# A graph network kernel: sums of the message pass kept in PSUM, one-hots made by GpSimd, and the first LayerNorm inside the pass

## What is computed

```python
# x (6250, 256), src/dst/edge_weight (100000,), dst sorted; row = src, col = dst
rbf = exp(-0.5 * ((d[:, None] - centers) / (abs(widths) + 1e-5)) ** 2) * env[:, None]
r = silu(rbf @ rbf_w1 + rbf_b1) @ rbf_w2 + rbf_b2
W = silu(silu(r @ filt_w1 + filt_b1) @ filt_w2 + filt_b2) @ filt_w3 + filt_b3
agg = segment_sum((x[col] @ node_w + node_b) * W, row)          # the message pass
o = layernorm(x + agg) * ln_g + ln_b
x = layernorm(x + o * sigmoid(o @ gate_w + gate_b))             # the node stage
fwd = segment_sum(w * x[col, :128], row) / clip(deg_row, 1)
bwd = segment_sum(w * x[row, 128:], col) / clip(deg_col, 1)
out = layernorm(x + concat([fwd, bwd]))
```

## Time and profile before

| | us |
|---|---|
| median of 3 runs (5069.38 to 5073.18) | 5071.47 |
| the profiled execution | 5067.16 |
| its span, first to last instruction | 5065.1 |

### The profile page before, as it was taken

The page is one execution under the profiler, slowest core; times in us unless marked ns, Lnnn a source line. Parts: engine busy times, 40 slices in busy tenths (PEclk is TensorE's granted clock), DMA queues, the critical chain, the costliest instruction groups (busy, mean ns, idle before and its releaser), DMA issues.

```text
span 5065.1 us, 77985 instructions
## 1 busy us (share of the span) xinstructions
PE 3600.8 (71%) x16432; PEld 2653.5 (52%) x16433; DVE 2815.1 (56%) x7139; ACT 2019.5 (40%) x5492; POOL 3207.5 (63%) x3263
## 2 busy tenths in 40 slices
PE   6999999999999999788875544444443556565662
PEld 4655555555555555466653344444443555555552
DVE  4665656556566565466668522222222666666667
ACT  1555455554555545488884211111111222222221
POOL 0777777777777777600003477777777777777772
PEclk8999999999999999999997655555555776777775
DMA  7544444444444444476661111111111433334334
GB/s 191 134 136 135 135 138 136 137 135 135 137 135 136 135 135 138 137 226 216 215 212 40 32 53 53 53 53 53 53 53 59 113 102 102 102 105 107 102 102 77
DMA packets 464444, 588.32 MB, mean 116 GB/s; under 512 B 70163, under 2 KB 385171, under 8 KB 464406
## 3 DMA queue, kind: packets, MB, share of 16 engines
q0 software_dynamic: 128512, 317.64, 20.5%
q1 hardware_dynamic: 335894, 270.26, 18.9%
HBM read 391.39 MB, written 196.22 MB: 116 GB/s over the span
## 4 chain that ended last, share of the span: by engine, by line
POOL 41%; issue 23%; PE 12%; DVE 11%; DVEq 5%; DMA 4%; ACT 2%; POOLq 1%; SPq 0%; ACTq 0%
POOL s_rows L495 14%; POOL d_rows L528 14%; POOL arena L487 12%; DVE arena L1369 5%; DMA arena<-s_rows 3%; DVEq L313 3%; PE ps L908 3%; PE ps L989 3%; PE ps L980 2%; DVE agg L1234 1%; PE ps L933 1%; DVEq L1369 1%; DVE arena L1318 1%; ACT arena L643 1%; POOLq L287 1%
## 5 line engine op out<-in xcount | busy, mean ns | idle before, releaser
L528 POOL DMA_INDIRECT d_rows<-arena,adr x832 | 809.7, 973 | 302.8 <-issue 253.1
L487 POOL DMA_INDIRECT arena<-y_rows,idx x784 | 754.5, 962 | 354.2 <-issue 238.6
L541 POOL DMA_INDIRECT arena<-x_half,idx x832 | 808.2, 971 | 253.5 <-issue 250.2
L495 POOL DMA_INDIRECT s_rows<-arena,adr x784 | 770.4, 983 | 245.7 <-issue 244.8
L869 PE MATMUL ps<-f3s,arena 128*128 128x256 f32 x3136 | 728.2, 386 | 129.1 <-ACT arena L587 129.0
L958 PE MATMUL ps<-agg,arena 128*128 x1664 | 430.0, 440 | 521.7 <-ACT arena L699 521.6
L858 PE MATMUL ps<-arena,f2s 128*128 128x512 f32 x1568 | 706.1, 593 | 0.0
L869 PEld LDWEIGHTS ps<-f3s,arena 128*128 128x128 f32 x3136 | 581.1, 190 | 233.8 <-issue 120.9
L958 PEld LDWEIGHTS ps<-agg,arena 128*128 128x128 f32 x1664 | 370.0, 328 | 575.6 <-issue 575.6
L1369 DVE TENSOR_TENSOR arena<-arena,ps 128x129 f32 x1664 | 481.0, 289 | 333.0 <-issue 87.4
L989 PE MATMUL ps<-arena 128*128 128x129 f32 x1664 | 338.2, 367 | 425.4 <-issue 261.9
(11 more groups left out here) (195 smaller groups left out, 5850.9 us busy)
## 6 DMA issues: line engine op xcount, KB each, us to landing
arena<-s_rows SPq DMA_DIRECT2D x52, 2088.0 KB, 8.4
arena<-d_rows SPq DMA_DIRECT2D x52, 1040.0 KB
arena<-wrow SPq DMA_DIRECT2D x392, 64.0 KB
arena<-env_row SPq DMA_DIRECT2D x392, 64.0 KB
d_rows<-arena,adr POOLq DMA_INDIRECT x832, 2.3
arena<-x_half,idx POOLq DMA_INDIRECT x832, 2.5
s_rows<-tpl_s SPq DMA_DIRECT2D x98, 130.5 KB, 7.0
arena<-y_rows,idx POOLq DMA_INDIRECT x784
```

Source lines behind the costliest of these rows:

```text
L487: pool.indirect_dma_start(gath[b][:, t, :], None, y_rows, bass.IndirectOffsetOnAxis(ap=idx[b][:, t:t + 1], axis=0)).then_inc(gathered[b], 16)
L495: pool.indirect_dma_start(s_rows, bass.IndirectOffsetOnAxis(ap=adr[b][:, t:t + 1], axis=0), msg[b][:, t, :], None).then_inc(scattered[b], 16)
L528: pool.indirect_dma_start(d_rows, bass.IndirectOffsetOnAxis(ap=adr[b][:, t:t + 1], axis=0), drow[b][:, t, :], None).then_inc(scattered_d[b ...
L541: pool.indirect_dma_start(gath2[b][:, t, :], None, x1_half, bass.IndirectOffsetOnAxis(ap=idx[b][:, t:t + 1], axis=0)).then_inc(gathered2[b ...
```

## The change

- The sums of the message pass stay in PSUM. Four banks take the blocks in turn; every product is accumulated (`start=False`) into its block's bank, at an offset that TensorE reads from the new table `slot_of` into a register. Before a group TensorE also waits, with the group's block number from a second register, until that block's bank is free.
- VectorE no longer adds every tile. When a block's last tile is multiplied (table `ends`), `take_out` adds the bank to x, which has been loaded into `agg` during the edge stage, and clears the bank. After seven blocks VectorE normalises the chunk and applies gain and shift.
- GpSimd makes all one-hots, by a compare of the lane numbers with the tile's column. ScalarE only copies the records.
- `s_rows` is loaded in chunks of 8 tiles into four buffers.
- Square roots of both LayerNorms become an integer start value and three Newton steps on VectorE.
- In the node stage TensorE turns chunk c + 1 ahead of the gate product of chunk c; `tr_c` and `gate_c` have two buffers each.
- Every block has at least one tile, and `SR` is shorter.

The diff, cut to its core:

```diff
-SR = ST + TAIL + NB
+SR = ST + NB
...
+PT = 8
+PC = ST // PT
...
-        s_buf = [take(CT, RW) for _ in range(2)]
-        hot = [take(GT, P) for _ in range(2)]
-        apart = take(GT, P)
+        s_buf = [take(PT, RW) for _ in range(4)]
+        hot = [take(GT, P) for _ in range(4)]
+        apart = [take(GT, P) for _ in range(2)]
         node_at = at
-        x_c = [take(CB * H) for _ in range(3)]
-        h_c = [take(CB * H) for _ in range(3)]
+        resid = take(NB * H)
+        h_c = [resid[:, c * CB * H:(c + 1) * CB * H] for c in range(CHUNKS)]
         at = 0
-        tr_c, gate_c, res_c = take(CB * H), take(CB * H), take(CB * H)
+        tr_c, gate_c = [take(CB * H) for _ in range(2)], [take(CB * H) for _ in range(2)]
...
+            sp.wait_ge(table_mm, 2)
+            sp.dma_start(agg_n[:, 0:2, :], x_n[:, 0:2, :]).then_inc(x_in, 16)
...
+                sp.dma_start(agg_n[:, bass.ds(i, 1), :], x_n[:, bass.ds(i, 1), :]).then_inc(x_in, 16)
...
-                if not (fixed(c) and c < 2):
-                    hold(sp, agg_mm, 8 * c - 8)
-                    sp.wait_ge(rec_kept, c - 1)
-                sp.dma_start(s_buf[b], s_v[:, bass.ds(c * CT, CT), :]).then_inc(s_in[b], 16)
...
+                if not (fixed(c) and c < 4):
+                    hold(sp, agg_mm, PT * c - 3 * PT + 1)
+                    sp.wait_ge(rec_kept, c - 3)
+                sp.dma_start(s_buf[b], s_v[:, bass.ds(c * PT, PT), :]).then_inc(s_in[b], 16)
...
+            loop(sp, load_messages, PC, 4, 4, 0)
+            for c in range(CHUNKS):
...
-            for c in range(CHUNKS):
-                h = by_block(h_c[c % 3])
-                pool.wait_ge(affine, c + 1)
-                G.tensor_tensor(h, h, gb[:, 0:1, :].to_broadcast([P, CB, H]), ALU.mult).then_inc(gained, 1)
-                pool.wait_ge(gained, c + 1)
-                G.tensor_tensor(h, h, gb[:, 1:2, :].to_broadcast([P, CB, H]), ALU.add).then_inc(normed, 1)
+
+            def one_hot(g, q, b):
+                c2, j = b // 2, b % 2
+                if j == 0:
+                    hold(pool, s_in[c2], 16 * q + 16)
+                if not (fixed(g) and g < 4):
+                    hold(pool, agg_mm, GT * g - 3 * GT + 1)
+                for t in range(BY_ACT, GT):
+                    last = G.tensor_scalar(hot[b % 4][:, t, :], lane[:, :], s_buf[c2][:, j * GT + t, H:H + 1],
+                                           None, ALU.is_equal)
+                last.then_inc(hotp_done, 1)
+
+            loop(pool, one_hot, G1, 8, 8, 0)
...
-            def one_hot(g, q, b):
-                c2, j = b // 4, b % 4
-                if j == 0:
-                    act.wait_ge(s_in[c2], 16 * q + 16)
-                    A(rec[:, bass.ds(g * GT, CT), :], s_buf[c2][:, :, H:H + RF], ACT.Copy).then_inc(rec_kept, 1)
-                if not (fixed(g) and g == 0):
-                    act.wait_ge(hots_done, g)
-                for t in range(GT):
-                    last = A(apart[:, t, :], lane[:, :], ACT.Square, scale=-1.0,
-                             bias=s_buf[c2][:, j * GT + t, H:H + 1])
-                last.then_inc(apart_set, 1)
-                act.wait_ge(apart_set, g + 1)
-                if not (fixed(g) and g < 2):
-                    act.wait_ge(agg_mm, 2 * g - 2)
-                A(hot[b % 2], apart, ACT.Relu, scale=-1.0, bias=ones[:, 0:1]).then_inc(hots_done, 1)
-
...
+            def keep(c, q, b):
+                act.wait_ge(s_in[b], 16 * q + 16)
+                A(rec[:, bass.ds(c * PT, PT), :], s_buf[b][:, :, H:H + RF], ACT.Copy).then_inc(rec_kept, 1)
+
+            loop(act, keep, PC, 4, 4, 0)
+            act.wait_ge(rec_kept, PC)
...
+            for k in range(SLOTS):
+                last = mm(ps[:, 4 + k, 0:H], ident[:, :], f2s[:, 0, :], start=True, stop=False, skip_group_check=True)
+            last.then_inc(banks_open, 1)
+            slots = ps[:, 4:4 + SLOTS, :].rearrange("p a b -> p (a b)")
...
-                pe.wait_ge(hots_done, g + 1)
-                if not (fixed(g) and g < 4):
-                    pe.wait_ge(added, GT * g - 3 * GT)
+                at = nc.values_load_multi_w_load_instructions(
+                    slot_of[0:1, bass.ds(g * GT, GT)], [mybir.EngineType.PE], min_val=0, max_val=(SLOTS - 1) * 512,
+                    skip_runtime_bounds_check_because="a number's last two bits, times 512")[1]
+
+                block_no = pe.value_load(slot_of[32:33, bass.ds(g * GT + GT - 1, 1)], min_val=1, max_val=NB)
+                pe.wait_ge(slot_free, block_no)
+                pe.wait_ge(hotp_done, g + 1)
                 for t in range(GT):
-                    last = mm(ps[:, 2 * (b % 4) + t // 2, (t % 2) * H:(t % 2 + 1) * H], hot[b % 2][:, t, :],
-                              s_buf[b // 4][:, (b % 4) * GT + t, 0:H], start=True, stop=True)
-                    if t % 2:
-                        last.then_inc(agg_mm, 1)
-
+                    mm(slots[:, bass.ds(at[t], H)], hot[b % 4][:, t, :],
+                       s_buf[b // 2][:, (b % 2) * GT + t, 0:H], start=False, stop=False,
+                       skip_group_check=True).then_inc(agg_mm, 1)
+
+            pe.sem_inc(agg_mm)
             loop(pe, aggregate, G1, 8, 8, 0)
-            pe.wait_ge(added, GT * G1)
-
...
+            turn_node(0)
+            pe.wait_ge(slot_free, SLOTS + NB)
             for c in range(CHUNKS):
-                node_products(c)
+                if c + 1 < CHUNKS:
+                    turn_node(c + 1)
+                gate_node(c)
...
+                if f == 0:
+                    step(V.tensor_scalar(ends[:, :], start[:, :], 1.0, None, ALU.add))
+                    step(V.memset(ends[:, NB - 1:NB], ST + 1))
...
+                    for k in range(2):
+                        for p, off in ((32, 0.0), (0, -1.0)):
+                            last = V.tensor_scalar(slot_of[p:p + 1, k * (ST // 2):(k + 1) * (ST // 2)],
+                                                   ps[p:p + 1, 5 + k, 0:ST // 2], off, None, ALU.add)
+                    step(last)
+                    last = V.tensor_scalar(slot_of[0:1, :], slot_of[0:1, :], SLOTS - 1, 9,
+                                           ALU.bitwise_and, ALU.logical_shift_left)
...
-            V.memset(agg[:, :], 0.0).then_inc(agg_zero, 1)
-            dve.wait_ge(agg_zero, 1)
-
-            def add_up(g, q, b):
-                places = places_of(mybir.EngineType.DVE, 0, g, H)
-                for t in range(GT):
-                    if not (fixed(g) and g == 0 and t == 0):
-                        dve.wait_ge(added, GT * g + t)
-                    dve.wait_ge(agg_mm, 2 * g + t // 2 + 1)
-                    rows_of = agg[:, bass.ds(places[t], H)]
-                    V.tensor_tensor(rows_of, rows_of, ps[:, 2 * (b % 4) + t // 2, (t % 2) * H:(t % 2 + 1) * H],
-                                    ALU.add).then_inc(added, 1)
-
-            loop(dve, add_up, G1, 8, 8, 0)
-            dve.wait_ge(added, GT * G1)
-
...
+            step = stepper(nv)
+
+            def inverse_root(of):
+
+                step(V.tensor_scalar(var_eps[:, :], of[:, :, 1], EPS_LN, None, ALU.add))
+                step(V.tensor_scalar(halved[:, :], var_eps[:, :].bitcast(i32), 1, None, ALU.logical_shift_right))
+                step(V.tensor_scalar(rstd[:, :].bitcast(i32), halved[:, :], -1.0, float(RSQRT), ALU.mult, ALU.add))
+                for _ in range(3):
+                    step(V.tensor_tensor(newton[:, :], rstd[:, :], rstd[:, :], ALU.mult))
+                    step(V.scalar_tensor_tensor(newton[:, :], newton[:, :], -0.5, var_eps[:, :], ALU.mult, ALU.mult))
+                    step(V.scalar_tensor_tensor(rstd[:, :], newton[:, :], 1.5, rstd[:, :], ALU.add, ALU.mult))
+
+            def normalise(to, src):
                 for j in range(CB):
...
+                    last = V.tensor_scalar(by_block(to)[:, j, :], by_block(src)[:, j, :], mv[:, j, 0:1],
+                                           rstd[:, j:j + 1], ALU.subtract, ALU.mult)
+                return last
...
+            dve.wait_ge(banks_open, 1)
+            for k in range(SLOTS):
+                V.memset(ps[:, 4 + k, 0:H], 0.0).then_inc(slot_free, 1)
+
+            def take_out(n):
+                last_tile = dve.value_load(ends[0:1, n:n + 1], min_val=1, max_val=ST + 1)
+                dve.wait_ge(agg_mm, last_tile)
+                bank = ps[:, 4 + n % SLOTS, 0:H]
+                V.tensor_tensor(resid[:, n * H:(n + 1) * H], agg[:, n * H:(n + 1) * H], bank, ALU.add).then_inc(summed, 1)
+                dve.wait_ge(summed, n + 1)
+                V.memset(bank, 0.0).then_inc(slot_free, 1)
...
+            for c in range(CHUNKS):
+                for j in range(CB):
+                    n = c * CB + j
+                    take_out(n)
+                    last = V.bn_stats(stats[:, j, :], resid[:, n * H:(n + 1) * H])
                 step(last)
...
                 for j in range(CB):
                     last = V.bn_aggr(mv[:, j, :], stats[:, j, :])
```

(77 more changed lines are left out.)

121 lines of the change are left out of this document (27 added, 94 removed).

## The result

| | before | after |
|---|---|---|
| median of 4 runs each, same chip, us | 5070.43 (5067.46 to 5073.18) | 5127.38 (5125.97 to 5130.46) |
| the profiled execution's span, us | 5065.1 | 5126.6 |

The change makes the kernel slower: the ratio is 1.0115, with a 95% interval of 1.0103 to 1.0128. I had forecast 4877, 250 us less. The times of four stages tell where these 250 us are; the first and last start of one line of each stage stand in its row.

The account below looks back on a forecast made before the run. GpSimd's indirect DMAs bound edges, back and forth; ScalarE's one-hots paced the message pass. Message pass and node stage end 194 us earlier: 5067.16 minus 194 is 4873, median 4.3 above, 4877; range 4825 to 4975.

Parts of the forecast that it names:

- One-hots on GpSimd: Message pass: four GpSimd compares per group at 0.36 us each, 1.44 us, 1.6 with waits; bounds 0.25 to 0.6.
- rival (A): Message pass bound by GpSimd's compares; at 0.55 us each 83 us more, 4960; chance 0.19 short of break-even, 0.05 beyond.
- T1: Message pass: time of one GpSimd compare, taken as 0.36 us; a group costs 4 T1 + 0.15 if GpSimd bounds.
- the 2139 that I had named as a sign of being wrong altogether: Edge stage: the forecast is wrong altogether if the edges end later than 2139.
- The break-even at a group of 2.88: Message pass: at 2.88 us a group the whole 194 us gain is gone, a compare of 0.68 us.
- Nothing is given back: After the node stage: 9.7 us to the first scatter stays, and both GpSimd stages follow unchanged.
- PE: Message pass: TensorE and its sequencer set 1.95 us a group, 406 us for 208 groups; bounds 1.76 to 2.3.
- rival (B): Message pass: TensorE's register loads don't overlap its array, 3.1 us a group, 239 us more, 5116; chance 0.05.
- The 11 us that increments one after another would add: Message pass, TensorE: 416 more semaphore increments serialized at 26.3 ns each, by the Trainium skill, an estimated 11 us later.
- Node stage: Node stage: VectorE the bound at 11.8 us per chunk, ending 96 us after the message pass, at 2652.7.
- rival (C): Node stage: the clock sags to half and the stage takes 50 us longer, 4927; chance 0.07.
- rival (D): Message pass: banks don't get free in time because GpSimd shuts VectorE out; with the rest about 5000, chance 0.02.

Follow-up runs that it names:

- the 32 fillers: The changed kernel with 32 idle one-column memsets of an unused tile on VectorE right before its forth-stage loop: 4976.35 us, ratio 0.9807 to the kernel before.
- the pair of loop lengths: Kernel with 64 idle VectorE memsets, plus twelve idle semaphore increments per group in VectorE's forth loop: 6553.83 and 6579.68 us against 6376.38 and 6424.65 without, slow chips.

## Why the prediction was wrong, step by step

**The term "One-hots on GpSimd" was mis-sized; rival (A) came.** I took T1 = 0.36 between a select of 0.29 and a copy's 2.0 ns per column. It is 0.577, and 0.605 with the waits for VectorE, at the far end of the bounds. The slope was about right (1.6 ns a column measured, 2.0 taken); what failed is the "start of some 0.1": a copy of 784 columns says nearly nothing about the fixed part of an operation, and the select at 0.29 is another instruction. With T1 = 0.605 my own formula, 4 T1 + 0.15, gives 2.57 us a group; measured are 2.42, since GpSimd had no waits of its own. The pass took 502.6 us instead of 406 + 4 for the clock, and began at 2151.9, 5.4 later than I had it: 93 + 5 are the 98 us. Of the 5.4, one is the compares'. The rest is the end of the edges: by the chain that ended last, the last scatter landed at 2143.6, against 2139.1 before, which is past the 2139 that I had named as a sign of being wrong altogether. It is worth only 4.4 us, and it moves from run to run (2137.5 with two groups at once); the shorter first load did save its 3 us (5.37 in place of 8.63). The break-even at a group of 2.88 fits, since at 2.42 half of the 194 us were left. As a time of one compare it isn't 0.68, though: without the waits of 0.15 an estimated 0.72.

**"Nothing is given back" was wrong, and no rival had it.** 145 us went into the forth stage and 12.5 behind its last gather, from the place of VectorE's code. Both terms together, 98 + 157, are the 255 us between the span I had in the sum (4871.1) and 5126.6. I had asked of the later stages only whether their operations changed. The profile of before showed the queue of instructions with 24 packets, and I didn't use it. With the 32 fillers 151 of these 157 us came back, 156 by the ratios.

**What held.** *PE:* 1.95 us a group forecast, 2.02 measured where nothing else set it (two tiles by ScalarE), 15 us over the pass; that the loads run partly under the matmuls is right, so rival (B) is out: no 3.1 us. The 11 us that increments one after another would add aren't seen: where two groups are loaded at once, passes with an increment on every second are 0.219 us apart. *Node stage:* 95.1 against 96 us. L1269's seven starts, 2667.2 to 2738.1, are 11.82 us apart (forecast 11.8), and the twelve steps of a root start 0.2 apart:

```profile
2674.32 0.17 DVE L1221 TENSOR_SCALAR var_eps<-mv 128x7 f32<-128x7 f32 x1
...
2676.54 0.17 DVE L1227 SCALAR_TENSOR_TENSOR rstd<-newton,rstd 128x7 f32<-128x7 f32 x1
2676.74 1.06 DVE L1231 TENSOR_SCALAR agg<-arena,mv,rstd 128x256 f32<-128x256 f32 x3
```

*Clock:* 0.89 in the node stage, not 0.73 as in the earlier trace rows; rival (C) is out. *Banks:* in the pass VectorE waited 393.6 us for TensorE and TensorE never for a bank; rival (D) is out. The 9.7 us to the first scatter and the back stage's pace are as forecast. With both failed terms taken away, the kernel with ScalarE's one-hots and the fillers takes 4889, 12 us above the forecast (16 by the ratio); its pace is ScalarE's 1.98, so that this comes so near is partly luck. Of the contention between VectorE and GpSimd I had only the one direction, VectorE waiting: it was the other that cost, 18 us. What the Newton steps or the first LayerNorm in the pass bring by themselves wasn't measured apart.

## What to carry to other kernels

Where many small operations move to another engine, its fixed cost per instruction decides, and a large operation's time per column says nothing of it: bound it from an operation of the same kind and size, or take the bad end as likely. When instructions are added or removed ahead of a long loop, look at the packets of the instruction queue in both profiles; a stall by "issue" once per turn was cured by some idle instructions in front, and by the pair of loop lengths a shorter body should do it too. Before work is moved off an engine that seems to set the pace, take its idle gaps out first: here ScalarE was fast enough in the new pass with its deeper buffers. Deeper buffers in the old pass weren't run.

## What the runs showed of the hardware

- The same 285 VectorE instructions per turn took 1057 to 1063 us or 1204 to 1206 us over the stage, by their place in the program modulo 128 instructions (the runs at the usual pace); each turn with a stall has five fetches of 8192 bytes and some 5.5 us of standstill.
- A compare of 128 x 32 on GpSimd takes 0.43 us and one of 128 x 128 0.58: by these two, an estimated 0.38 us is there at any width.
- A GpSimd compare of 0.6 us took 2.13 us beside a two-input operation of VectorE of 2.07 us; that one was 0.05 us longer than the same operation without GpSimd at work.
- Loading the places of two groups at once, with one count of blocks and one wait for both, took TensorE's group from 2.02 to 1.75 us, although the loads run beside the matmuls.
- ScalarE makes the four one-hots of a group in 1.93 us, and in 2.05 with the copy of the records.
